# A two-layer transformer kernel: the down weights' Hadamard turn as two products with a row exchange through DRAM

## The reference, cut to what matters

```python
x = L0_attn_x                                # (2, 1024, 512) float32, 2048 tokens
xn = _layernorm(x)
x = x + _L0_attn_ref(xn, ...) + _L0_ffn_ref(xn, W1, W2, W3)
xn = _layernorm(x)
x = x + _L1_attn_ref(xn, ...) + _L1_ffn_ref(xn, ...)

def _L0_ffn_ref(x, W1, W2, W3):              # hidden size 2048
    hidden = jax.nn.silu(x @ W1.T) * (x @ W3.T)
    hidden = fwht(hidden)                    # fast Walsh-Hadamard transform, scaled by 1/sqrt(2048)
    return hidden @ W2.T
```

## Time and profile before

| | |
|---|---|
| median of 3 runs | 1920.17 us (1918.46 to 1922.30) |
| profiled execution | 1918.47 us |
| its span | 1916.7 us, 24850 instructions |
| mean granted TensorE clock | 0.951 of full |
| TensorE busy | 1732.4 us, 90% |
| VectorE busy | 1097.4 us, 57% |
| ScalarE busy | 735.2 us, 38% |
| GpSimd busy | 298.0 us, 16% |
| moved by DMA | 153.44 MB, mean 80 GB/s |

### The profile page before, as it was taken

One profiled execution on the slowest core, in us unless ns is written; L12 is line 12 of the kernel. 1 busy time (PEld: TensorE's weight loads), 2 busy tenths in 40 slices (PEclk: granted clock), 3 DMA queues, 4 the chain that ended last, 5 costly groups with the idle time before them and its releaser, 6 DMA issues. The chain is left out here.

```text
span 1916.7 us, 24850 instructions
## 1 busy us (share of the span) xinstructions
PE 1732.4 (90%) x8396; PEld 1402.2 (73%) x8396; DVE 1097.4 (57%) x1868; ACT 735.2 (38%) x1527; POOL 298.0 (16%) x232
## 2 busy tenths in 40 slices
PE   4685999999999976997999899976899999999997
PEld 3464877777778865885777677765678888888885
DVE  6742245536532254256999899975455656656553
ACT  4421112211111232136999899973222221212121
POOL 4111111111021003020000000006502113203200
PEclk9876999999999987998999999997899999999998
DMA  6242011101010013962344444418200010001011
GB/s 223 88 154 83 17 34 39 39 28 44 16 40 17 34 44 123 274 263 93 106 126 129 124 131 132 132 31 283 88 1 27 7 34 33 33 0 33 11 44 44
DMA packets 81482, 153.44 MB, mean 80 GB/s; under 512 B 8281, under 2 KB 33241, under 8 KB 80226
## 3 DMA queue, kind: packets, MB, share of 16 engines
q1 hardware_dynamic: 81378, 152.16, 25.5%
HBM read 101.80 MB, written 50.33 MB: 79 GB/s over the span
## 5 line engine op out<-in xcount | busy, mean ns | idle before, releaser
L1747 DVE TENSOR_TENSOR pt_lo<-p_turn,pt_hi 128x512 fp32r<-128x512 f32 (+3 forms) x384 | 201.1, 551 | 24.7 <-ACT pt_hi L1722 18.4
L1740 DVE TENSOR_REDUCE row_top<-p_score 128x1 f32<-128x128 f32 (+7 forms) x256 | 189.6, 750 | 20.9 <-PE p_score L1674 20.7
L1714 ACT ACTIVATE prob<-p_score,row_top 128x128 f32<-128x128 f32 (+7 forms) x256 | 189.6, 744 | 8.3 <-DVE row_top L1740 6.2
L1722 ACT ACTIVATE pt_hi<-p_turn 128x512 fp32r<-128x512 f32 (+3 forms) x384 | 181.8, 492 | 11.9 <-issue 4.5
L1685 PE MATMUL p_turn<-ident,prob 128*128 128x128 f32 x1152 | 182.8, 277 | 2.9 <-DVE pt_lo L1747 2.7
L1187 DVE TENSOR_TENSOR hid<-hid,p_up 128x512 f32<-128x512 f32 x64 | 44.0, 687 | 222.6 <-PE p_up L711 201.7
L1700 PE MATMUL p_o<-pt_hi,v 128*128 128x512 f32 (+3 forms) x384 | 149.2, 396 | 4.2 <-ACT o_both L1730 3.4
L1685 PEld LDWEIGHTS p_turn<-ident,prob 128*128 128x128 f32 x1152 | 132.9, 142 | 16.8 <-DVE pt_lo L1747 3.5
L1672 PE MATMUL p_score<-stack 128*128 128x512 f32 (+3 forms) x384 | 129.5, 392 | 14.3 <-PEq L53 7.0
L295 DVE TENSOR_TENSOR ff_hid<-ff_hid,ff_p_up 128x512 f32<-128x512 f32 x64 | 43.8, 685 | 162.4 <-PE ff_p_up L184 161.2
L948 ACT ACTIVATE hid<-p_gate 128x512 f32<-128x512 f32 x64 | 38.1, 598 | 253.2 <-PE p_gate L711 253.1
(11 more groups left out here) (248 smaller groups left out, 4092.3 us busy)
## 6 DMA issues: line engine op xcount, KB each, us to landing
stack<-qk_parked SPq DMA_DIRECT2D x256, 128.0 KB, 4.0
qk_parked<-qk SPq DMA_DIRECT2D x16, 1024.0 KB, 3.9
raw<-in_wgu SPq DMA_DIRECT2D x32, 256.0 KB, 2.9
v_parked<-v_out SPq DMA_DIRECT2D x16, 512.0 KB, 5.2
v<-v_parked SPq DMA_DIRECT2D x8, 1024.0 KB, 9.2
o_parked<-o_both SPq DMA_DIRECT2D x64, 128.0 KB
o<-o_parked SPq DMA_DIRECT2D x8, 1024.0 KB, 8.9
ff_raw_gu<-in_wgu SPq DMA_DIRECT2D x16, 512.0 KB, 4.0
```

What stands on the lines that cost most here:

```text
L1714: act.activation(prob[r // QB][:, h % 2, r % QB, 0:width_of(r)], p_score[:, r % 2, 0:width_of(r)], ACT.Exp, bias=top[:, r:r + 1], accum_ou ...
L1722: act.activation(pt_hi[:, (BL * h + j) % PT, c0:W], p_turn[:, (BL * h + j) % TB, c0:W], ACT.Copy).then_inc(rounded, 1)
L1740: dve.tensor_reduce(top[:, r:r + 1], p_score[:, r % 2, 0:width_of(r)], AX_X, ALU.max, negate=True).then_inc(topped, 1)
L1747: dve.tensor_tensor(pt_lo[:, slot, c0:W], p_turn[:, (BL * h + j) % TB, c0:W], pt_hi[:, slot, c0:W].bitcast(F32), ALU.subtract).then_inc(sp ...
```

## The change

- The turn is made in two products, with a 16-row by 128-row regrouping between them. The slice is loaded with rows p x 16 + c. Product 1 is with the 128x128 Hadamard matrix; its result (4 products of 128x512 per slice, copied by ScalarE over the slice itself) is stored to a DRAM tensor `half_turned` and loaded back with the rows exchanged; product 2 is with a 16x16 Hadamard matrix crossed with an 8x8 identity. The butterflies on GpSimd and VectorE go. In all there are 32 float32 products in 16 pairs (which, slice, half).
- Pairs (1,0,0) and (1,0,1) stand ahead of everything on TensorE; one of the other 14 stands before each half-chunk from (unit 0, c 0, j 1) to (unit 1, c 3, j 0).
- Group 0's down weights no longer go through DRAM: ScalarE's copy of the first bank of each slice is the rounded d_hi, VectorE makes d_lo from PSUM (`first_rest`, new), and TensorE waits for it before the second pair of the slice in product 2. The blocks of groups 1 to 3 are stored (three quarters of a slice). The gate and up columns are permuted on the host to match.
- Four slices have four buffers, two of them the unused last quarter of x_hi and x_lo, whose layout becomes quarter, k, 512. So quarter 3 of x is turned in unit 2, after those slices have been stored.
- The low-rank product becomes weights-first: per quarter 12 matmuls of 24 rows x 512 columns, a copy, four transposes, a copy to `low_p` (`low_keep`, new), in units 2 and 3; `set_up` and `turn_wide` are in unit 3.
- The second moments aren't measured; the variance of the normed x is worked out from the first (`second_var`), once for all tokens.
- In ScalarE's and VectorE's orders items 4 to 7 of group 0's weights stand inside unit 0 (c 0 and c 1), behind silu and product.
- SP's order is new, as below; all ten-row operands of the mixer have nine rows.

```diff
             load_x(0)
+            sp.dma_start(turn_w[:], t["turns"]).then_inc(turn_in, 16)
+            load_slice(0)
             sp.dma_start(ident[:], t["eye"]).then_inc(eye_in, 16)
             for k in range(RING):
                 load_raw(k)
...
+            load_x(1)
+            for s in range(1, SL):
+                load_slice(s)
+            store_half(0)
+            load_raw(3)
+            load_x(2)
+            load_half(0)
+            load_raw(4)
+            load_x(3)
+            load_raw(5)
+            store_n1(0)
+            load_raw(6)
+            reload_x(0)
+            load_raw(7)
...
+            store_n1(1)
+            store_half(1)
+            load_half(1)
+            store_half(2)
+            load_half(2)
+            reload_x(1)
+            store_half(3)
+            load_half(3)
+            store_n1(2)
+            store_n1(3)
+            store_slice(0)
+            store_slice(1)
+            reload_x(2)
+            store_slice(2)
+            store_slice(3)
```

```diff
+            def rotate(which, s, h):
+                n = 2 * turn_number(which, s, h)
...
+                if h == 0:
+                    pe.wait_ge((slice_in if which == 1 else half_in)[s], 16)
+                for i in range(2):
+                    m = 2 * h + i
+                    if n:
+                        pe.wait_ge(rot_copied, n + i - 1)
+                    if which == 2 and s and h == 0 and i == 0:
+                        pe.wait_ge(d_first, s)
+                    if which == 2 and h == 1 and i == 0:
+                        pe.wait_ge(d_first, s + 1)
+                    pe.matmul(p_out[:, i], turn_w[:, which - 1], rot[s][:, 4 * m:4 * m + 4].rearrange("p n d -> p (n d)"),
                               start=True, stop=True).then_inc(rot_done, 1)
...
+            def first_rest(s):
+                dve.wait_ge(rot_copied, 2 * turn_number(2, s, 0) + 1)
+                cols = slice(SW * s, SW * s + SW)
+                dve.scalar_tensor_tensor(d_lo[:, :, cols], p_out[:, 0].rearrange("p (n d) -> p n d", n=NC), ROOT,
+                                         d_hi[:, :, cols].bitcast(F32), ALU.mult, ALU.subtract).then_inc(d_first, 1)
```

ScalarE's order (`ACT`), where the copies stand:

```diff
+            root(1, quarter(0))
+            norm(0, 0)
             gu_round(0)
             gu_round(1)
-            root(1, quarter(0))
-            norm(0, 0)
+            rot_copy(1, 0, 0)
+            rot_copy(1, 0, 1)
+            x_round_quarter(0, 0)
             gu_round(2)
-            x_round_quarter(0, 0)
             gu_round(3)
-            root(2, quarter(0))
-            root(3, quarter(1))
+            root(2, quarter(1))
             norm(1, 0)
-            for k in range(4, 8):
-                gu_round(k)
             for u in range(UNITS):
...
+                    for turn_of in turns_before(u, c, 0):
+                        rot_copy(*turn_of)
                     silu(u, c)
+                    if u == 0 and c < 2:
+                        gu_round(4 + 2 * c)
+                        gu_round(5 + 2 * c)
+                    for turn_of in turns_before(u, c, 1):
+                        rot_copy(*turn_of)
                     if c:
                         hi(u, c - 1)
```

More of the change, by code:

```diff
@@ L365, in layer_zero @@
         h_lo = nc.alloc_sbuf_tensor_at("h_lo", [P, 2, NC, W], F32R, offset=at)
[L366 to L373, removed]
+        d_hi = sb("d_hi", [P, NC, D], F32R)
+        d_lo = sb("d_lo", [P, NC, D], F32R)
+        late = nc.sbuf_base
+        sb("late_slab", [P, 2 * NCH * SW])
+        homes = spare + [late, late + 4 * NCH * SW]
+        rot = [nc.alloc_sbuf_tensor_at(f"rot{i}", [P, NCH, SW], F32, offset=homes[i]) for i in range(SL)]
         skip = nc.alloc_sbuf_tensor_at("skip", [P, D], F32, offset=late)
@@ L544, in _ @@
             sp.dma_start(tok[0:R + 1, 0], t["up_rows"]).then_inc(rows_in, 16)
-            load_raw(8 + RING)
+            for s in range(2):
+                sp.wait_ge(rot_out[s], 16)
             sp.wait_ge(up_split, 1)
@@ L548, in _ @@
             load_tok(1)
-            for k in range(12, 23):
+            for k in range(8 + RING, 19):
                 load_raw(k)
@@ L552, in _ @@
                 load_tok(i)
-            for k in range(23, 27):
+            for k in range(19, 23):
                 load_raw(k)
@@ L556, in _ @@
                 load_tok(i)
-            for k in range(27, 35):
+            for k in range(23, 31):
                 load_raw(k)
@@ L560, in _ @@
                 load_tok(i)
-            for k in range(35, 39):
+            for k in range(31, 35):
                 load_raw(k)
@@ L564, in _ @@
                 load_tok(i)
-            for k in range(39, 48):
+            for k in range(35, 44):
                 load_raw(k)
@@ new lines, in low_rank @@
+            def low_rank(q):
+                if q == 0:
+                    pe.wait_ge(fold_done, 1)
+                    pe.wait_ge(x_split, KD * QUARTERS)
+                else:
+                    pe.wait_ge(low_copied, q)
+                o = p_side[0:3 * R, 0]
+                for k in range(KD):
+                    pe.matmul(o, fold_r[:, k, 0], x_hi[:, q, k], start=(k == 0), stop=False)
+                    pe.matmul(o, fold_r[:, k, 0], x_lo[:, q, k], start=False, stop=False)
+                    mm = pe.matmul(o, fold_r[:, k, 1], x_hi[:, q, k], start=False, stop=(k == KD - 1))
+                mm.then_inc(low_done, 1)
@@ L680, in set_up, with turn_low @@
+            def turn_low(q):
+                pe.wait_ge(low_copied, q + 1)
+                if q:
+                    pe.wait_ge(low_kept, q)
+                for j in range(J):
+                    mm = pe.transpose(p_side[:, 1, 3 * R * j:3 * R * (j + 1)], low[0:3 * R, j * P:(j + 1) * P],
+                                      ident[0:3 * R, 0:3 * R])
+                mm.then_inc(low_turned, 1)
             def set_up():
-                pe.wait_ge(low_added, 1)
+                pe.wait_ge(low_copied, QUARTERS)
@@ L986, in _ @@
                         if c == 0:
-                            root(2 * QUARTERS + q + 1, quarter(q))
+                            root(5 + q, quarter(q))
                         if c == 2:
@@ L1019, in _ @@
             for q in range(1, QUARTERS):
-                root(3 * QUARTERS + q + 1, quarter(q))
+                root(9 + q, quarter(q))
                 norm(q, 1)
@@ L1070, in x_rest @@
             def x_rest(q, last, ks=range(KD)):
+                if q == 3 and not last:
+                    dve.wait_ge(rot_out[1], 16)
                 for k in ks:
                     dve.wait_ge(x_round, KD * (QUARTERS * last + q) + k + 1)
-                    cols = slice(q * W, (q + 1) * W)
-                    dve.tensor_tensor(x_lo[:, k, cols], bank_of(q, k, last), x_hi[:, k, cols].bitcast(F32),
+                    dve.tensor_tensor(x_lo[:, q, k], bank_of(q, k, last), x_hi[:, q, k].bitcast(F32),
```

455 lines of the change are left out of this document (223 added, 232 removed).

## The result

The changed kernel takes 1887.12 us (median of four runs, 1885.98 to 1888.48) against 1920.01 us before (four runs on the same chip, 1918.46 to 1922.30): a ratio of 0.9828, 95% interval 0.9811 to 0.9845, so 32.9 us less. The forecast was 1888.5. The profiled execution took 1887.56 us, 30.9 less than the profiled one of before (1918.47).

What follows compares the result with a forecast made beforehand. TensorE was taken as the bound from 178.5 us, waiting on ScalarE and GpSimd earlier. Starting the output product 53 us sooner, less 18.1, 3.2 and 1.8 behind it, gives 30: 1918.5 - 30 = 1888.5 us, range 1872 to 1908.

Steps and rivals of the forecast that it cites:

- Bound: TensorE is the bound from 178.5 to 300 us; time saved ahead of that reaches the end one for one.
- the mark: Start of unit 0's output product on TensorE, 178.49 us before the change; forecast at 125.5, 53 us sooner.
- Behind the mark: After the output product begins: moved work adds 18.1 us, low_keep waits 3.2, cold restarts a net 1.8.
- (a): Weight loads on SP's queue: item 3 lands at 30.7 us instead of 19.92, item 5 at 40.5.
- (b): ScalarE and VectorE chain after item 3: 12.2 us, pair (1,1,1) starts at 43, TensorE idles some 10.
- (c): Unit 0 from 43 us: half-chunks, pairs, transposes, one cold restart and waits take 36.9 us, ending at 80.
- (d): Unit 1 up to the mark: half-chunks, pairs, transposes and 8.2 us of waits take 45.3 us.
- two more cold restarts: Low-clock restarts of TensorE behind the mark: 3.5 us, against 1.7 for the one at the mark, which goes.
- Late weights: Rival, chance 0.19: slower weight loads, or a late block near unit 4, leave a gain of 20 us: 1898.
- Fewer waits: Rival, chance 0.15: ScalarE and VectorE run ahead in units 0 and 1, loads are quicker; gain 42 us: 1876.
- The clock rival: Rival, chance 0.07: TensorE stays at 1.2 GHz from 43 us to the mark, adding 60 us: 1948.
- no effect: Rival, chance 0.03: TensorE's extra 15 us and new waits eat the whole gain; within 4 us of before.

Runs made afterwards that it cites:

- e1: Changed kernel with weight item 3 loaded behind slice 1 instead of behind all four slices and the first half-turned store: 1886.55 us.
- e5: Changed kernel with group 0's down blocks again stored to DRAM, loaded back and split by GpSimd, without first_rest: 1891.0 us.
- e8: Changed kernel with e6's reorderings, further ScalarE copies early, x parking later in SP's queue, half of x quarter 1's split earlier: 1854.12 us.
- e7: Changed kernel with the low-rank products in their old form (x as weights, 48 and 24 columns) at the new place: 1892.42 us.
- e6: Changed kernel with item 3, copy (1,1,0), first_rest and low_keep moved earlier, a root and a norm one chunk later: 1865.35 us.
- e4: Changed kernel with half-turned slices 1 to 3 each stored twice, their loads waiting for both stores: 1887.0 us.
- e3: Changed kernel with VectorE's first_rest placed ahead of product and lo of the same chunk instead of behind them: 1876.63 us.

## Why the prediction was right

**Bound.** Right: what the mark gains reaches the end, less what was moved behind it. Behind the mark the change leaves 1757.4 us of span, e1 to e5 1756.4 to 1759.5, and e8, with 2.8 us of waits for `low_keep` less, 1754.8. Two lie off: e7 with 1761.2, where the clock fell, and e6 with 1750.4, which is 4.2 less than the same 2.8 us explain; that I can't place.

**(a) Loads.** Item 3 was rounded from 29.64 instead of 30.7. DMA from 18 to 28 us in 40 slices of time, the loads of the turn's slices up to 25.5 and then the first store of the exchange:

```profile
GB/s 295 291 291 289 291 293 291 289 287 293 291 289 295 277 299 287 295 291 289 293 291 285 293 293 285 293 291 287 287 319 350 348 348 344 350 346 346 336 344 338
```

The rate of the earlier trace rows held for loads of 512-byte runs too, at 290 GB/s. The store behind them moved at 336 to 350, so it took 3.0 us and not 3.6: those are the 0.6 us by which the trace stands ahead of my 30.2. The stores of slices 2 and 3, from 65 and 78 us on, moved at 290 again; what sets the two rates apart isn't shown. By the estimate from the Trainium skill (DMA: Bandwidth & Descriptors, "Why small descriptors are slow (HBM only)") item 3 would have come at 27.8; the trace doesn't bear that ratio out for the loads, with 290 against 379 GB/s a factor of 1.31 and not 1.13.

**(b) The chain.** Priced 12.2, measured 12.24 (29.64 to 41.88). The idle stretch was to be 10 and was 13.5, since the first two half-chunks were done at 28.4 and not at 33: only one of the two pairs at the head ran cold, and x_lo was there by 20.9. It cost nothing at the mark, as the chain ends when it ends.

**(c) Unit 0.** Priced 36.9, measured 39.7 (41.88 to 81.56, where the wait ahead of 83.71 begins). The waits are 5.3 for the 5.4 priced. The term that was mis-sized is the clock: one restart at 1.7, and there were 4.7 us in two (3.0 and 1.7), for the slow stretch goes on behind the cold pair into its half-chunk.

**(d) Unit 1.** Priced 45.3, measured 46.9. The waits are 8.4 for 8.2. The clock again, 1.7 us behind the wait at 108.18, was priced at nothing. Mark: 128.4 for 125.5. (My terms add up to 30.7 + 12.2 + 36.9 + 45.3 = 125.1; the 125.5 on record is 0.4 too high.)

**Behind the mark.** Priced 23.1, measured 19.2. The low-rank products took 11.1 for 10.9 at 0.23 us each, so the row of equal columns was the right one of three; fewer rows in use gave nothing back. Transposes 1.4 for 2.4, set-up 2.4 for 2.7, x transposes 1.8 for 2.1, `low_keep` 2.8 for 3.2. The step that failed is "two more cold restarts": the grant was 1.00 from the mark to 215 us, though the waits were there. These measured terms, less the 1.7 of the restart that goes, make 17.8; 1.4 us are not placed. So I had the clock too good ahead of the mark by 4.7 us and too bad behind it by 3.5. The mark gained 50.1 us for the 53 priced, and 19.2 were given back for the 23.1: two errors of 2.9 and 3.9 us that cancel, and the sum was 1.4 us off the median by luck in part. The mechanism, waits by the order of ScalarE and VectorE with the exchange under cover, came as described.

**Rivals.** Late weights: no; e1 shows item 5 as the next one late, with a margin of 1.2 us for the 1 us given, and from the mark to 250 us no wait of TensorE is for a weight. Fewer waits: no, they came as priced. The clock rival's price is not borne out either: 6.4 us instead of 60, with a grant of 0.94 from 45 to 126 us. The exchange is hidden (e4), and the gain of 33 us rules out no effect. The Trainium skill (TensorE: Matmul & The Clock Gate, "Part 1: The HAM clock gate") has the throttled clock as the default that activity must release. By that rule, the trace agrees for the stretch behind 41.88 us; that every wait costs twice was my own reading, which the section doesn't state, and it isn't so, since the waits of 2.15 us at 83.71 and 121.14 cost no clock and the one at 108.18 did.

**VectorE's short operations** took 0.16 to 0.20 us, as said, with GpSimd idle beside them.

**What the change left.** It gained 33 us and put its own copies and `first_rest` behind other work; 33 more lay in the order alone (e8).

## What to carry to other kernels

Where an engine works through a written order, look for an instruction that frees PSUM or a buffer for the bound engine and stands behind one that waits for a transfer: move it ahead, then look at the next one, as one alone gives back only its own share (in this kernel 4.6 us at the mark for one copy, 29.8 for all the orders of e8). A part that replaces one wait by several short ones can be worth almost nothing until these stand right: the blocks kept on the chip gave 1.3 us at the mark in one order and 11.3 in the other. Judge it only after its own waits are ordered away.

## What the runs showed of the hardware

- A wait of 2.15 us of TensorE cost clock at one of three places in the run after the change, and at other places in others of the same order: the pair behind it took 2.95 us at 118.02 in e1, and 2.66 at 83.05 in e7. Taking 7.1 us of such waits away gave 10.0 (e3).
- In one run (e7), a TensorE that was busy all the time didn't keep its full clock: bursts of matmuls of 24 and 48 columns, 0.11 us apart, were followed by a grant of 0.50 for 5 us and 0.90 over 89 us, with no idle time at all; with the form of 512 columns in the same place the grant was 1.00 (after the change).
- A matmul with 24 of 128 weight columns in use took the same as one with 128: 0.23 us for 512 columns (146.56 to 146.79 after the change).
- Loads of 512-byte runs moved at 290 GB/s, and so did most stores; the first store of the exchange moved at 336 to 350.
